# Convolution in 32x32 TensorE tiles, on pairs of batch tiles, in a two-layer conditioned feed-forward kernel

## The reference, cut to what matters

```
# layer 0: grouped convolution along the row (9 taps, pad 4, 4 groups of 8 channels), plus a bias per (batch, channel)
y  = conv(x, weight, groups=4) + (c @ c_weight.T)[:, :, None] + bias[None, :, None]
# 8-bit product: each row of y and of the 512x512 weight is scaled by its largest magnitude / 127 and rounded
x1 = x + round(y / a) @ round(w / s).T * a * s
# layer 1: a 32x32 matrix and a bias per batch, mixed by a softmax over 8 of them from a small two-layer net on c
z  = agg_w[b] @ x1[b] + agg_b[b]
out = x1 + scale * (z @ (2 * kernel - 1))      # kernel is boolean 512x512
```

## Time and profile before

| | us |
|---|---|
| three runs | 137.9, 138.81, 139.2 |
| median | 138.81 |
| span of the profiled execution, first to last instruction | 136.1 |
| TensorE busy in it | 126.1 |
| VectorE, ScalarE, GpSimd busy | 76.0, 32.1, 54.1 |

### The profile page before, as it was taken

One profiled execution on the slowest core, in us unless ns is written; L12 is line 12 of the kernel. 1 busy time (PEld: TensorE's weight loads), 2 busy tenths in 40 slices (PEclk: granted clock), 3 DMA queues, 4 the chain that ended last, 5 costly groups with the idle time before them and its releaser, 6 DMA issues.

```text
span 136.1 us, 2630 instructions
## 1 busy us (share of the span) xinstructions
PE 126.1 (93%) x858; PEld 74.1 (54%) x858; DVE 76.0 (56%) x169; ACT 32.1 (24%) x58; POOL 54.1 (40%) x66
## 2 busy tenths in 40 slices
PE   6899849999879999999999999999999999997990
PEld 6682246272446464655555555656464737375870
DVE  5323598195084565565656474747474738384742
ACT  0000436549551112212130303030303030305010
POOL 5725080043543434343444435353626261725300
PEclk9999995995999999999999999999999999999999
DMA  3999999003993496868687787788787764232023
GB/s 110 209 254 288 239 224 209 2 0 91 235 236 67 162 209 193 203 187 200 175 214 192 194 200 185 203 182 223 163 242 149 244 147 146 29 125 77 2 90 141
DMA packets 13734, 22.61 MB, mean 166 GB/s; under 512 B 2216, under 2 KB 2952, under 8 KB 13728
## 3 DMA queue, kind: packets, MB, share of 16 engines
q1 hardware_dynamic: 11680, 20.99, 61.5%
q10 hardware_dynamic: 1984, 1.48, 4.8%
q0 software_dynamic: 64, 0.07, 0.2%
HBM read 18.32 MB, written 4.19 MB: 165 GB/s over the span
## 4 chain that ended last, share of the span: by engine, by line
PE 88%; DMA 3%; DVE 2%; issue 2%; ACT 1%; ACTq 1%; DVEq 0%
PE ps L326 33%; PE ps L343 11%; PE ps L364 11%; PE ps L370 11%; PE ps L354 10%; DMA cond_w_raw<-in_L_cond_c_weight_dram 3%; PE ps L334 3%; PE ps L306 1%; PE ps L280 1%; PE ps L255 1%; PE ps L287 1%; PE ps L260 1%; PE ps L315 1%; ACT aggb_bc L630 1%; DVE rounded L522 1%
## 5 line engine op out<-in xcount | busy, mean ns | idle before, releaser
L735 POOL TENSOR_TENSOR x<-xr,delta 128x512 f32<-128x512 f32 x15 | 17.5, 1166 | 51.9 <-DVE res L536 38.3
L326 PE MATMUL ps<-x,conv_st 128*32 128x512 f32 x256 | 32.6, 629 | 0.7 <-issue 0.7
L637 ACT ACTIVATE z_hi<-z 128x512 fp32r<-128x512 f32 x16 | 10.1, 630 | 73.9 <-DVE z L543 73.9
L511 DVE TENSOR_REDUCE row_max<-ps 128x1 f32<-128x512 f32 x16 | 11.0, 689 | 25.5 <-PE ps L326 25.4
L742 POOL TENSOR_TENSOR z_lo<-z,z_hi 128x512 fp32r<-128x512 f32 x15 | 19.2, 1284 | 8.2 <-ACT z_hi L637 8.2
L364 PE MATMUL ps<-sign,z_hi 128*128 128x512 f32 x64 | 20.1, 436 | 0.3 <-issue 0.2
L354 PEld LDWEIGHTS ps<-mix,x 128*128 128x128 f32 x128 | 16.5, 191 | 2.3 <-ACT mix L624 0.8
L370 PE MATMUL ps<-sign,z_lo 128*128 128x512 f32 x64 | 17.5, 395 | 0.0
L343 PE MATMUL ps<-wq,xq 128*128 128x512 f16 x64 | 16.6, 382 | 0.9 <-ACT xq L643 0.9
L354 PE MATMUL ps<-mix,x 128*128 (+1 forms) x128 | 17.1, 276 | 0.0
L326 PE MATMUL ps<-x,conv_last 128*32 128x512 f32 x128 | 16.6, 592 | 0.0
(11 more groups left out here) (90 smaller groups left out, 88.8 us busy)
## 6 DMA issues: line engine op xcount, KB each, us to landing
x<-in_x_dram SPq DMA_DIRECT2D x48, 256.0 KB, 5.1
xr<-in_x_dram SPq DMA_DIRECT2D x16, 256.0 KB, 2.9
out_dram<-res SPq DMA_DIRECT2D x16, 256.0 KB, 2.8
q_raw<-in_L_ffn_weight_dram ACTq DMA_DIRECT2D x2, 512.0 KB, 10.2
sign_raw<-in_L_ffn_kernel_dram ACTq DMA_DIRECT2D x1, 256.0 KB, 9.2
w_sb<-in_L_cond_W_dram POOLq DMA_DIRECT2D x1, 64.0 KB, 7.5
w_sb<-in_L_cond_W_dram ACTq DMA_DIRECT2D x1, 64.0 KB, 11.3
cond_raw<-in_cond_dram ACTq DMA_DIRECT2D x1, 32.0 KB, 3.2
```

The lines of the kernel that those rows point to most:

```text
L326: mm = pe.matmul(Y[s][C * b:C * (b + 1), :], w, x3[:, s, b, JS * m:JS * m + L], start=(m == 0), stop=(m == MS - 1), tile_position=(0, C * b))
L511: dve.tensor_reduce(row_max[:, s:s + 1], Y[s], AX_X, ALU.max, apply_absolute_value=True)\
L735: nc.gpsimd.tensor_tensor(x1_slot(k, par - 2), xr[:, s, :], delta[:, s, :], ALU.add)\
```

## The change

- The convolution uses that the 4 groups couple only 8 channels with 8: a half r of 16 input channels and 16 output channels is a block of its own. x stands in two copies (`xs`), interleaved channel by channel on the partitions, the second shifted by one column. Moving every second column gives 2 taps per step and 2 outputs (even and odd) per weight column: 5 steps m, 256 columns, and each instruction is a 32x32 piece of the array, `tile_position=(32 r, 32 j)`. Two tiles (t even and odd) take the row groups 0, 1 and 2, 3: sixteen pieces side by side. Each row group writes a PSUM bank of its own.
- The bias is no longer a matmul row: ScalarE evicts the convolution from PSUM to `ysb` and adds it (`convolved`). VectorE takes the maxima from `ysb`; since a row's even and odd outputs stand on two partitions, seven small instructions (`scales`, two of them partition shuffles) do the scales of two tiles at once.
- The transposes put the rows back in order by a permuted identity and a strided output; PSUM `TURN`, `ACC`, `Z` and `FIN` are one bank each (the convolution has four), `x1` six deep, `xr`, `res`, `ysb`, `rounded` four, `z_hi` and `z_lo` three.
- The second product of a tile comes in step t+5 instead of t+3, the first in t+2, the mixing in t+3. No hardware loop: everything is written out. Loads of small weights are spread over the SP and POOL queues, the first weight comes in four loads.

```diff
-            def conv_tile(k, off):
-                t, half, s = tile(k, off)
-                pe.wait_ge(x3_in[s], 16 * JS * (half + 1))
-                pe.wait_ge(bias_rows, t + 1)
-                need(pe, quant_done, t - 1)
-                for m in range(MS):
-                    for b in range(NB):
-                        w = conv_st[:, m, :] if m < MS - 1 else conv_last[:, s, b, :]
-                        mm = pe.matmul(Y[s][C * b:C * (b + 1), :], w, x3[:, s, b, JS * m:JS * m + L],
-                                       start=(m == 0), stop=(m == MS - 1), tile_position=(0, C * b))
+            def conv_inputs(t):
+                pe.wait_ge(x_in[slot(t)][t % 2], 32 * (t // (2 * NX) + 1))
+                need(pe, y_ready, t - 1)
+            def conv_step(t, m):
+                h = t % 2
+                for r in (2 * h, 2 * h + 1):
+                    for j in range(NB):
+                        mm = pe.matmul(Y[r][C * j:C * (j + 1), :],
+                                       conv_st[C * r:C * (r + 1), m].rearrange("k o p -> k (o p)"),
+                                       xs[C * r:C * (r + 1), slot(t), j, SH * m:SH * m + L - 1:SH],
+                                       start=(m == 0), stop=(m == MS - 1), tile_position=(C * r, C * j))
+            def conv_pair(t):
+                conv_inputs(t)
+                conv_inputs(t + 1)
+                for m in range(MS):
+                    conv_step(t, m)
+                    conv_step(t + 1, m)
...
# TensorE, the order
+            for t in range(4, NT + 5):
+                if t % 2 == 0 and t < NT:
+                    conv_pair(t)
+                if 2 <= t - 2 < NT:
+                    turn_tile(t - 2)
+                if 0 <= t - 5:
+                    ffn1_tile(t - 5)
+                if t in (5, 6, 7):
+                    spread_bias(t - 4, t - 2)
+                if 2 <= t - 2 < NT:
+                    ffn0_tile(t - 2)
+                if 1 <= t - 3 < NT:
+                    mix_tile(t - 3)
...
# VectorE
+            def scales(t, n):
+                q, hs = t // 2 % 2, slice(t % 2, t % 2 + n)
+                flat = lambda a: a[:, q, hs, :].rearrange("r h g -> r (h g)")
+                done = t + n
+                dve.wait_ge(max_done, done)
+                dve.stream_shuffle(flat(row_swap), flat(row_max), [i ^ 1 for i in range(32)]).then_inc(swap_done, n)
+                dve.wait_ge(swap_done, done)
+                dve.scalar_tensor_tensor(out=flat(row_both), in0=flat(row_max), scalar=QMAX * TINY, in1=flat(row_swap),
+                                         op0=ALU.max, op1=ALU.max).then_inc(both_done, n)
...
+            def quantise(t):
+                q, h = t // 2 % 2, t % 2
+                dve.wait_ge(cinv_done, t + 1)
+                need(dve, turn_done, t - 3)
+                for g in range(2):
+                    last = dve.tensor_scalar(rounded[:, t % 4, g, :], ysb[:, t % 4, g, :], c_inv[:, q, h, g:g + 1], ROUND,
+                                             ALU.mult, ALU.add)
+                last.then_inc(quant_done, 1)
...
+            for t in range(4, NT + 5):
+                if t % 2 == 0 and t < NT:
+                    maxima(t)
+                if t - 5 >= 0:
+                    result(t - 5)
+                if t % 2 == 0 and t < NT:
+                    maxima(t + 1)
+                    scales(t, 2)
+                if 2 <= t - 2 < NT:
+                    dequantise(t - 2)
+                if t < NT:
+                    quantise(t)
+                if 1 <= t - 3 < NT:
+                    mix_bias(t - 3)
...
# ScalarE
+            def convolved(t):
+                act.wait_ge(conv_done, t + 1)
+                act.wait_ge(bias_copied, 1)
+                need(act, quant_done, t - 3)
+                for g in range(2):
+                    last = act.activation(ysb[:, t % 4, g, :], Y[2 * (t % 2) + g], ACT.Identity,
+                                          bias=bias_col[:, g, t:t + 1])
+                last.then_inc(y_ready, 1)
...
+            for t in range(4, NT + 5):
+                if t % 2 == 0 and t < NT:
+                    convolved(t)
+                if 2 <= t - 2 < NT:
+                    quantised(t - 2)
+                if t % 2 == 0 and t < NT:
+                    convolved(t + 1)
+                if t in (5, 6, 7):
+                    spread_bias(t - 4)
+                if 1 <= t - 3 < NT:
+                    high_part(t - 3)
...
# GpSimd
+            for t in range(4, NT + 5):
+                if 2 <= t - 2 < NT:
+                    first_sum(t - 2)
+                if 1 <= t - 3 < NT:
+                    low_part(t - 3)
```

More of the change, by code:

```diff
@@ L128, in adaln_ffn @@
[L128 to L136, removed]
@@ L237, in _ @@
+            for t in range(2, NT + 6):
+                if t % 2 == 0 and t + 4 < NT:
+                    load_x(t + 4)
+                    load_x(t + 5)
+                if 4 <= t + 1 < NT:
+                    load_rows(t + 1)
+                if 0 <= t - 6 < NT:
+                    store(t - 6)
+            for s in range(4):
+                sp.wait_ge(stored[s], 16 * (NT // 4))
         @block.tensor
         def _(pe):
-            pe.wait_ge(warm_set, 1)
-            for n in range(WARM[0]):
-                pe.matmul(ACC[:, 0:P], ones[:], ones[:], start=True, stop=True)
@@ L336, in turn_tile, with ffn0_tile @@
                 mm.then_inc(turn_done, 1)
-            def ffn0_tile(k, off):
-                t, half, s = tile(k, off)
+            def ffn0_tile(t):
                 pe.wait_ge(xq_ready, t + 1)
@@ new lines, in _ @@
+            mm.then_inc(ctx_ready, 1)
+            warm(WARM[2])
+            pe.wait_ge(conv_copied, 2)
+            conv_tile(0)
+            hidden1()
+            hidden2()
+            pe.wait_ge(ident_h_ready, 2)
+            ffn0_weights(0)
+            logits()
+            ffn0_weights(1)
+            ffn0_weights(2)
+            ffn0_weights(3)
+            pe.wait_ge(conv_copied, 3)
+            conv_tile(1)
+            ffn0_scales()
+            attention()
+            pe.wait_ge(wsc_ready, 1)
@@ new lines, in _ @@
+            softmax_first()
+            for a in range(1, LC):
+                ffn0_round(a)
+            dve.wait_ge(low_high_ready, 1)
+            maxima(0)
+            scales(0, 1)
+            quantise(0)
+            softmax_second()
+            ffn0_scales()
+            attention_copy()
+            maxima(1)
+            scales(1, 1)
+            quantise(1)
+            mixed_bias()
+            mixing_weights()
+            dequantise(0)
+            maxima(2)
+            maxima(3)
@@ L627, in spread_bias @@
             def spread_bias(n):
-                for q in (n, n + 1):
-                    act.wait_ge(bc_mm, q + 1)
-                    act.activation(aggb_bc[:, NT // NQ * q:NT // NQ * (q + 1), :].rearrange("p t r -> p (t r)"),
-                                   BC[q % 2], ACT.Copy).then_inc(bc_copied, 1)
-            def high_part(k, off):
-                t, half, s = tile(k, off)
-                act.wait_ge(z_ready, t + 1)
-                need(act, ffn1_done, t - 1)
-                act.activation(z_hi[:, s, :], z[:, s, :], ACT.Copy).then_inc(hi_ready, 1)
@@ L667, in _, with high_part @@
-            steps(act, 2, step, 3)
+                act.activation(xq[:, t % 2, :], TURN, ACT.Identity, bias=half_col[:, 0:1])\
+                   .then_inc(xq_ready, 1)
+            def high_part(t):
+                act.wait_ge(z_ready, t + 1)
+                need(act, ffn1_done, t - NH + 1)
+                act.activation(z_hi[:, t % NH, :], z[:, t % 2, :], ACT.Copy).then_inc(hi_ready, 1)
+            conv_repeat()
+            convolved(0)
+            hidden(0, b0_in, b0_col[:, 0:1])
+            hidden(1, b1_in, b1_col[:, 0:1])
```

764 lines of the change are left out of this document (359 added, 405 removed).

## The result

The changed kernel takes 163.56 us (median of four, 162.44 to 164.47) against 139.0 for the kernel before (137.9 to 139.26) on the same chip: a ratio of 1.178, 95% interval 1.169 to 1.186. The forecast was 134.9, its range 127.5 to 144.5, so it was wrong in sign and in range. The profiled execution took 164.2 with a span of 162.4.

The account below looks back on a forecast made before the run. TensorE bound the kernel before; afterwards a chain through VectorE and ScalarE would set 12.45 us per pair. conv_pair(4) at 35.9, conv_pair(8) at 62.3, conv_pair(14) at 99.7, span 132.2, plus 2.7: 134.9 us, range 127.5 to 144.5.

Parts of the forecast that it names:

- each link of the chain: Pair period: TensorE's second product, VectorE up to z, ScalarE's z_hi and xq, TensorE's first product and mixing; about 12.45 us.
- its lower bound of 2.13: Convolution on TensorE: least time for a pair of tiles, 2.13 us, against 2.36 forecast.
- 16 starts of 7 ns (0.1) and one drain (0.1): 2.36 per pair: Convolution on TensorE: ten waves of sixteen passes, 2.17 us, plus starts and drain; 2.36 us per pair against 5.42.
- the four column groups behave exactly so: Convolution on TensorE: reason for taking the low end, row groups run side by side as column groups do; 2.36 us.
- Rival (a): Convolution on TensorE: tiles run in two waves of eight, not sixteen together, a pair 4.5 us; 147.4 us, chance 0.12.
- I take 0.6 for the second start and for GpSimd beside it: VectorE's rounding per tile: two 128x256 halves from SBUF take 0.5 us, raised to 0.6.
- they show at most 0.18 us: VectorE's rounding beside GpSimd: the earlier rows show at most 0.18 us of one engine blocking the other.
- Rival (b): VectorE and GpSimd block one another: rounding's second half waits for x1, rounding takes 1.7 us; 144.8 us, chance 0.09.
- Seven small instructions, 1.2: VectorE's scales of a pair: five dependent and two independent instructions, 1.2 us, bounds 0.9 and 1.7.
- First product and mixing at the full clock: TensorE at the end of the pair's chain: first product 0.97 us and mixing 0.89 us.
- Rival (e): TensorE's clock falls in the new gaps, once per two pairs costing some 1.5 x 5 us; 142 us, chance 0.04.
- (c): Small instructions and evictions at their upper ends, 1.5 us for the seven, 0.8 rounding; 138.8 us, no change, chance 0.15.

Follow-up runs that it names:

- Experiment 1: Changed kernel with ScalarE taking z_hi of tile t-3 behind xq of tile t-1 instead of ahead of it; median 149.55 us.
- experiment 11: Against experiment 8, all convolution steps of tile t come ahead of those of t+1, eight pieces side by side; 149.61 us, ratio 1.075.
- experiment 2: Changed kernel with GpSimd's first sum waiting until VectorE has rounded the tile of the same step; median 156.75 us, ratio 1.123.
- experiment 8: Changed kernel with z_hi behind xq, GpSimd's first sum after rounding, row scales moved behind mixing's bias, 24 head fillers; median 135.85 us, ratio 0.983.
- 5: Changed kernel with the convolution on upper 16 bits of x and weights, one pass per instruction, changing the computation; 145.03 us in one execution.
- experiment 12: Against experiment 8, neighbouring convolution instructions alternate between two row groups; ratio 0.981, over ten executions median 139.28 us with before at 138.76.

## Why the prediction was wrong

**Right.** What bounds the kernel before; that order on ScalarE, and not the sum on any engine, would set the period; each link of the chain; TensorE's idle before odd first products; z_hi waiting for z; and seven rows of the table above within 0.11 us. Experiment 1 shows the chain: changing one place in ScalarE's order moved the span by 13.3 us. Redone, two sums of the prediction are off by little: in the head 24.9, 0.3 and 1.9 make 27.1 and not 27.4, and starts 25 ns apart would by its own 5.8 periods have cost 9.5 us, not 8. No run shows its lower bound of 2.13.

**Convolution, "16 starts of 7 ns (0.1) and one drain (0.1): 2.36 per pair".** This is the largest failed term, +1.44 in the period shown: 1.17 at full clock (3.53 with its drain against 2.36), the rest from a start at half clock. The step that failed is "the four column groups behave exactly so". The earlier trace rows shows four starts in 0.03 us, once in 0.45 us; it says how close a few waiting passes can start, not how many a stream can keep up. The kernel before never asked for more than one pass per 0.11 us (24 in 2.71), the new one asks for one per 14 ns and gets one per 20 (3.14 over 160). Rival (a) had "more than 15 ns apart" as its sign, and later starts are mostly 16.7 apart, but its mechanism, waves of eight, is refuted by experiment 11 (4.25).

The Trainium skill, "TensorE: Matmul & The Clock Gate", gave both: "Measured speedup vs the span model" some 4 ns per further piece, and "Wait — 56ns, not 53.3ns?" a floor of 25 ns between starts. The trace has 7 ns at first, then mostly 16.7, and 20 on the average, so the first overstates the rate of this stream and the second understates it.

**Rounding, "I take 0.6 for the second start and for GpSimd beside it".** +0.82. The failed reading is "they show at most 0.18 us": the earlier trace rows has four roundings in 2.00 us from 18.66, and w_diag of 594 to 782 ns that start from 16.9 to 18.7. Three of the four w_diag had ended by 18.68. The last began with the first rounding, and the two took 0.78 and 0.65 us where their like take 0.60 and 0.50: a row with one overlap was read as four. Rival (b)'s mechanism, at a chance of 0.09, held whole: in the changed kernel the second half of the rounding takes 1.24 to 1.26 us in every tile from 4 on, and 0.34 when GpSimd is kept off (experiment 2).

**Seven small instructions, 1.2.** +0.45, within the bounds (0.9 to 1.7). Four of them, each of which needs the one before, start 0.27 us apart (118.17, 118.44, 118.71, 118.98), not 0.19 as in the earlier trace rows.

**First product and mixing at the full clock.** +0.71 in this period. Rival (e) said "once per two pairs would cost some 1.5 x 5"; it came in five periods running, and for 23.8 us in the head. I gave it 0.04, although I had myself put 2 us of idle into every pair and had the row of 30.60 before me, where the clock fell in the kernel before too.

**The sum.** Head 6.7 us late (conv_pair(4) at 42.63, not 35.9); in experiment 8, with the clock held, it comes at 35.31; five periods 4.0 each too long, 20; tail 3.5 longer (162.4 less 126.45, against 132.2 less 99.7). Together 30.2 us of span. Around the span lie 1.8, not 2.7, us. No single cause carries it: alone, experiment 1 takes 13.3 us off the span, 2 8.9, and 5, with another computation, 19.2, which leaves 143.2 against 136.1 before.

**The chances.** The rivals (a), (b), (c) and (e) were priced as alternatives, each with the rest as forecast. They all came in part, and they feed one another: a longer chain on VectorE lengthens TensorE's wait, the wait drops the clock, and the low clock lengthens the next convolution. A range from cases taken one at a time couldn't hold the sum.

**Stops for instructions.** They weren't in the forecast, which counted unrolling as the loss of some loop instructions. The changed kernel shows 1.3 us of them and experiment 1 5.8, with the same number of packets: I take it that the waits for xq hide the rest.

**Open.** That the stops are instruction loads rests on their fixed places in the program and on the times of the packets; no kernel with fewer instructions and the same work was run. What in the fp32 stream sets 16.7 ns, the weight load, the second pass of each instruction, its length or the queue, isn't told apart: experiment 12 excludes only the order of row groups. What makes the clock fall isn't settled either: long waits go with most of the falls, but experiment 11 fell without one. And the terms' shares are read from one period's chain: experiments 2 and 5 took out the rounding's and the convolution's alone, the latter with its stops and at the price of another computation; the seven small instructions were never taken out by themselves.

## What to carry to other kernels

Starts of a few waiting instructions say nothing of the rate that a stream keeps; when a change makes three times as many instructions and shortens each, bound the sum by a rate that the trace shows sustained. Once one engine's work shrinks, walk the in-order queues for one whole period and put every producer that the critical engine waits for ahead of work that it doesn't (here two lines moved gave 13 us of span). Price the rivals together as well as alone, since a new idle can cost TensorE's clock as well, in the head too. And look at the durations of known instructions, not only at the row of the clock, which can start late.

## What the runs showed of the hardware

- Sixteen 32x32 pieces, at full clock: the first sixteen fp32 passes start 7 ns apart, later ones mostly 16.7 ns, with gaps of 0.13 to 0.19 us between groups; a pair's 160 passes take 3.14 us with sixteen pieces, 4.25 with eight; 80 single passes of 16-bit data take 1.04.
- A VectorE instruction from SBUF to SBUF (128x256 fp32, 0.34 us) that starts beside GpSimd's 1.19 us addition ends 0.15 us behind it: up to 1.26 us.
- The granted clock fell to 0.50 for 3.4 us around five of six waits of TensorE of 2.9 to 3.7 us. In the head it was low for 23.8 us (TensorE busy for 17.66 of them), and with fillers (busy for 21.25) it stayed at 1.00; in experiment 11, with the same fillers, it was low for 30.7 us with TensorE busy for 29.00 of 30.60.
- The record of the granted clock can begin late: at 40.9 us in experiment 1, whose tile 0 took 4.52 us ahead of it where 2.52 is the time at full clock.
- In programs of some 1800 matmul records, twice those of before, TensorE stands still inside a convolution at fixed places, for 0.3 to 2.9 us, and goes on 1.2 to 1.8 us behind the end of a 16 KB instruction packet (24 of 24 stops).
